# Order tables step by step, one pass for both contexts' tails, direct maxima in the last tile, expert biases on DVE: an eight-tile fp32r transformer block on one Trainium2 core

## What is computed

```python
# first block
nx = layer_norm(x)
evidence = softmax(nx @ Wq @ (ctx @ Wk).T / 16) @ (ctx @ Wv)
combined = concat(nx, evidence, cond)                  # 768 wide
probs = softmax(combined @ router_W + router_b)        # 3 experts
h = silu(combined @ e_w1[e] + e_b1[e])                 # 512 wide each
routed = sum_e probs[e] * (h @ e_w2[e] + e_b2[e])
g = sigmoid(silu(combined @ gate_w1 + gate_b1) @ gate_w2 + gate_b2)
x = x + g * (routed @ out_w + out_b)
# second block: 16 heads of width 16 over the 154 context tokens
q = ada_ln(x, cond) @ Wq + bq ;  k, v = split(ada_ln(ctx, cond) @ Wkv + bkv)
x = x + softmax(q @ k.T / 4) @ v @ Wp + bp
```

## Time and profile before

| quantity | value |
|---|---|
| runs, us | 566.02, 567.95, 571.80; median 567.95 |
| profiled execution | 570.17 us, of which the span from first to last instruction is 568.30 |
| busy in the span | PE 475.6, PEld 425.1, DVE 284.8, ACT 208.5, POOL 180.0 us |
| mean granted TensorE clock | 0.919 of full speed |
| mean of one instruction | tanh (L813) 598 ns, high half (L821) 620 ns, low half (L1303) 1298 ns, DVE product (L1161) 686 ns |
| one addition of 128x256 on POOL (L1353) | 0.72 us |

### The profile page before, as it was taken

One profiled execution on the slowest core, in us unless ns is written; L12 is line 12 of the kernel. 1 busy time (PEld: TensorE's weight loads), 2 busy tenths in 40 slices (PEclk: granted clock), 3 DMA queues, 4 the chain that ended last, 5 costly groups with the idle time before them and its releaser, 6 DMA issues.

```text
span 568.3 us, 9457 instructions
## 1 busy us (share of the span) xinstructions
PE 475.6 (84%) x3572; PEld 425.1 (75%) x3572; DVE 284.8 (50%) x717; ACT 208.5 (37%) x436; POOL 180.0 (32%) x167
## 2 busy tenths in 40 slices
PE   3998995959999978999889899979997999675563
PEld 2877895948988877878878787879787988652433
DVE  4536337673763574237733872494257426526212
ACT  1342331235346324532355227522741362142050
POOL 0653411063252434214522353424243122201111
PEclk9998997979999989999999999978996999768686
DMA  8376001320200112232001000200010001002000
GB/s 280 103 295 241 10 1 37 79 57 8 49 3 23 36 38 77 80 89 74 20 23 38 20 22 5 49 6 22 13 45 0 23 22 36 21 2 52 24 0 20
DMA packets 20608, 29.03 MB, mean 51 GB/s; under 512 B 4818, under 2 KB 17618, under 8 KB 20308
## 3 DMA queue, kind: packets, MB, share of 16 engines
q1 hardware_dynamic: 19264, 24.49, 14.1%
q0 software_dynamic: 1008, 3.67, 2.0%
q10 hardware_dynamic: 292, 0.28, 0.3%
HBM read 17.87 MB, written 2.10 MB: 35 GB/s over the span
## 4 chain that ended last, share of the span: by engine, by line
PE 51%; DVE 19%; issue 16%; ACT 6%; POOL 5%; DMA 2%; SPq 1%; POOLq 0%; ACTq 0%; DVEq 0%
PE hidden_banks L1368 4%; PE hidden_banks L1375 4%; PE hidden_banks L1370 4%; PE hidden_banks L1369 4%; PE score_banks L1677 3%; PE score_banks L1375 3%; DVE head_maxima L1221 3%; PE value_bank L1693 3%; PE token_bank L1368 3%; PE value_bank L1696 2%; PE token_bank L1369 2%; PE token_bank L1370 2%; PE score_banks L1654 2%; DVE router_logits L1147 2%; DVE hidden L1161 2%
## 5 line engine op out<-in xcount | busy, mean ns | idle before, releaser
L1303 POOL TENSOR_TENSOR hidden_low<-hidden,hidden_high 128x512 fp32r<-128x512 f32 x56 | 72.7, 1298 | 160.3 <-ACT hidden_high L821 160.2
L1221 DVE TENSOR_REDUCE head_maxima<-score_banks 128x2 f32<-128x308 f32 x128 | 55.1, 474 | 42.1 <-PE score_banks L1654 41.9
L1368 PE MATMUL hidden_banks<-normed_high,hidden_w_high 128*128 128x256 f32 x224 | 68.1, 304 | 3.3 <-DVE context_w_tail L922 2.7
L875 ACT ACTIVATE exp_ring<-score_banks 128x512 f32<-128x512 f32 x96 | 52.8, 601 | 38.5 <-PE score_banks L1677 38.2
L1368 PE MATMUL token_bank<-expert_out_high,hidden_high 128*128 128x256 f32 x192 | 58.7, 306 | 8.6 <-issue 7.2
L1369 PE MATMUL hidden_banks<-normed_high,hidden_w_low 128*128 128x256 f32 x224 | 64.3, 287 | 0.0
L1370 PE MATMUL hidden_banks<-normed_low,hidden_w_high 128*128 128x256 f32 x224 | 64.2, 287 | 0.0
L1161 DVE SCALAR_TENSOR_TENSOR hidden<-hidden,hidden_banks 128x512 f32<-128x512 f32 x56 | 38.4, 686 | 50.5 <-ACT hidden L813 49.6
L1654 PE MATMUL score_banks<-pair_keys,query_stack 96*128 96x308 f32 x128 | 39.8, 372 | 25.5 <-DVE head_maxima L1221 17.9
L1369 PE MATMUL token_bank<-expert_out_high,hidden_low 128*128 128x256 f32 x192 | 56.5, 294 | 0.0
L1370 PE MATMUL token_bank<-expert_out_low,hidden_high 128*128 128x256 f32 x192 | 56.4, 294 | 0.0
(11 more groups left out here) (209 smaller groups left out, 1146.7 us busy)
## 6 DMA issues: line engine op xcount, KB each, us to landing
unit_weights<-units SPq DMA_DIRECT2D x7, 768.0 KB, 5.1
query_stack<-queries_high SPq DMA_DIRECT2D x128, 32.0 KB, 1.9
w_slice<-units POOLq DMA_DIRECT2D x7, 512.0 KB, 3.9
tokens<-x SPq DMA_DIRECT2D x8, 256.0 KB, 7.1
query_stack<-queries_low SPq DMA_DIRECT2D x64, 32.0 KB, 1.9
out<-tokens SPq DMA_DIRECT2D x8, 256.0 KB, 2.2
w_T<-folds SPq DMA_DIRECT2D x1, 1536.0 KB, 8.5
pair_keys<-keys_high SPq DMA_DIRECT2D x32, 38.5 KB, 1.9
```

The costliest lines, as they stand in the source:

```text
L875: nc.scalar.activation(E[:, w % ERING, :], S[:, ring_of[key][0], :], ACT.Exp).then_inc(scalar_score, 1)
L1221: v.tensor_reduce(MX[:, s, :, c], S[:, ring_of[key][0], 0:2 * CTX].rearrange("p (j n) -> p j n", j=2), AX.X, ALU.max).then_inc(vector_most, 1)
L1303: nc.gpsimd.tensor_tensor(SL[:, ring(t, u), :], TB[:, ring(t, u), :], raw(SH[:, ring(t, u), :]), ALU.subtract).then_inc(gpsimd_h, 1)
L1368: mm(out_, lh, rh, start=start, stop=False, skip_group_check=skip)
```

## The change

- **Order tables.** `PLAN`, `PLAN_OF` (by tile) and `SETUP` give each step a slot of its own; `DELAY` has numbers of its own for the last tile. The first tile starts at slot 5 instead of 12.
- **Loads and start.** The first load holds context 0 and the value weights alone; four dummy matmuls (`warm`) stand before the first real one. Second weights come in six loads. The batch 1 slices are loaded by SP instead of POOL.
- **Context tails.** A new step `vt` computes, once per unit and for both batch entries, the tails with 32-column weights, and separately the condition's row; `context_w` keeps the first 128 tokens only. For batch entry 1 it uses the score banks' ring.
- **Keys.** The constant rows come by one DMA per batch entry; keys and queries are copied two pairs at a time (12 and 4 x 3 DMAs). Context x_hat moves from DVE to POOL.
- **Router.** ACT subtracts the maximum by its bias and makes the sum; the subtraction and the sum leave DVE.
- **Expert biases.** `bias2` makes each expert's bias once as a tile. From the third tile on `init` starts the sum of experts on DVE with bias x probability, and the bias matmuls are left out, except for the gate's.
- **Outputs.** A stream shuffle doubles the outputs (`dup`) so that high and low half share a tile of 128 rows; DVE makes the low half instead of POOL; `proj` has 2 matmuls a group and one bias matmul per half. Tile 6 and tile 7 use tiles and banks of their own.
- **Last tile.** `unstack` copies the keys back while its experts run; `most` multiplies the queries (high and low) by them with three 32-row matmuls, without the stack; the maxima go into the scores by a selection matrix (one matmul more per score) and not by DMA; rows, sums and outputs are made in two halves, tokens are stored in two parts. `fill` places 14 groups of four dummy matmuls.

```diff
-FIRST = 12
+FIRST = 5
+PLAN = {
+    "dup": (36.6, 40.5), "za": -0.51, "step": 1.99, "z": 0.3, "h": 1.5, "p": 3.33, "again": -9.3, "vw": -56.6,
+    "ln": -0.16, "norm": 1.7, "low": 11.8, "att": 7.8, "prob": 9.2, "route": 12.1, "logit": 15.01, "res": 17.8,
...
+    "most": (21.9, 22.1, 23.6, 25.2, 25.5, 26.9, 27.4, 28.1), "row": (29.46, 39.8), "stack": (13.9, 16.4, 17, 18.6),
...
+            def context_tail(key):
...
+                for k in range(KC):
+                    for b in range(BATCH):
+                        mm(tail_bank(u)[32 * b:32 * b + 32, 0:UCOLS], LT[b][:, k, :], U[:, u % URING, KC + k, :],
+                           start=(k == 0), stop=(k == KC - 1))
+                    for b in range(BATCH):
+                        last = mm(tail_bank(u)[64 + 32 * b:96 + 32 * b, 0:UCOLS], CO[:, k, b:b + 1].to_broadcast([P, 32]),
+                                  U[:, u % URING, 2 * KC + k, :], start=(k == 0), stop=(k == KC - 1))
...
             def logit(key):
-                nc.scalar.activation(PR[:, t % 2, :, :], LG[:, :, :], ACT.Exp).then_inc(scalar_logit, 1)
+                for s in range(NSUB):
+                    last = nc.scalar.activation(PR[:, t % 2, s, :], LG[:, s, :], ACT.Exp, bias=RT[:, 0, s:s + 1],
+                                                accum_out=RT[:, 1, s:s + 1])
...
+            def init(key):
...
+                for e in range(EXPERTS):
...
+                    for s in range(NSUB):
+                        p, bias = PR[:, t % 2, s, e:e + 1], BX[:, e, :] if e < 2 else BX3[:, :]
+                        if e == 0:
+                            last = v.tensor_scalar(ACC[:, s, :], bias, p, None, ALU.mult)
+                        else:
+                            last = v.scalar_tensor_tensor(out=ACC[:, s, :], in0=bias, scalar=p, in1=ACC[:, s, :],
+                                                          op0=ALU.mult, op1=ALU.add)
...
-                        if u % 2 == 0 and i == 1:
+                        if u % 2 == 0 and i == 1 and (t < PLAIN or u == 0):
                             last = mm(bank, BSEL[:, j:j + 1].to_broadcast([P, P]), CB[:, :], start=False, stop=True, skip_group_check=True)
...
             def most(key):
...
+                if t == LAST:
...
+                    exact(bank, (QH[rows, f, columns], QL[rows, f, columns]), (keys_high, keys_low), True, True).then_inc(tensor_most, 1)
+                else:
+                    mm(bank, QS[0:STACK, c, P * s:P * s + P],
+                       KS[b][0:STACK, c, :, :].rearrange("p j n -> p (j n)"), start=True, stop=True).then_inc(tensor_most, 1)
...
+            def proj_part(t, s, groups):
...
+                for g in groups:
+                    mm(proj_bank(t, s), both[:, g, c], WPh[:, g, :], start=(g == 0), stop=False)
+                    last = mm(proj_bank(t, s), both[:, g, c], WPl[:, g, :], start=False, stop=(g == GROUPS - 1))
```

More of the change, by code:

```diff
@@ L225 @@
+    "gpsimd": {
+        "h": 0.6, "ln": 0.8, "qn": -0.2, "low": 1, "keyn": 1.4, "split": 1.9,
+    },
+    "sync": {
+        "query": 10.5, "row": -4.5, "proj": -3.6, "last": 0.5, "key": -0.2, "place": 10.8, "query_last": 6.1,
+        "row_last": -1.7, "stack_last": -2.6,
+    },
 }
 LOOP = 2 * NU
-P_LAG = 3.3
 AGAIN = TPB - 1
-LN_AT, NORM_AT, LOW_AT, ATT_AT, PROB_AT, ROUTE_AT, LOGIT_AT = 0.5, 1.2, 3.2, 7.8, 9.3, 10.7, 12.4
-RES_AT, QN_AT, SHIFT_AT, XHAT_AT, QX_AT, QLOW_AT, QUERY_AT = 2.0, 2.1, 2.9, 3.0, 3.2, 5.2, 5.8
@@ new lines, in schedule @@
+    place(0, ("cv", 0), ("ck", 0), ("cv", 1))
+    for name in ("ln", "silu", "group", "gsplit", "setup2", "bias1", "cb", "bq"):
+        place(SETUP[name], (name, 0))
+    for u in range(NU):
+        place(SETUP["unit"][u], ("unit", u))
+        place(SETUP["vw"][u], ("vw", 0, u))
+        place(SETUP["vt"][u], ("vt", u))
+    for name in ("norm", "low", "att", "prob", "route", "logit"):
+        place(SETUP[name], (name, 0))
+    for u in range(1, NU):
+        place(SETUP["w2"][u - 1], ("w2", u))
@@ new lines, in schedule @@
+    place(SETUP["ck"], ("ck", 1))
+    for i in range(MODS):
+        place(SETUP["mod"][i], ("mod", i))
+    for i in range(2):
+        for name in ("late", "split", "keyn", "keyx", "key", "fold"):
+            place(SETUP[name][i], (name, i))
+    for name in ("sel", "unstack"):
+        place(SETUP[name], (name, 0))
+    for i in range(2):
+        place(SETUP["bias2"][i], ("bias2", i))
+    for i in range(FILLS):
+        place(SETUP["fill"][i], ("fill", i))
+    for t in range(NT):
+        at = FIRST + LOOP * t
@@ L295, in block1 @@
         for h in range(2):
-            place(at + RAW_AT[h], ("raw", t, h))
-            place(at + SUM_AT[h], ("sum", t, h))
-        place(at + SUMS_AT, ("sums", t))
-        place(at + OUT_AT, ("out", t))
-        place(at + OUTL_AT, ("outl", t))
-        place(at + PROJ_AT, ("proj", t))
-    place(0, ("setup", 0), ("load", 0), ("ctx", 0), ("fold", 0), ("ln", 0), ("silu", 0), ("group", 0))
-    place(1.5, ("bias1", 0), ("gsplit", 0))
-    for u in range(NU):
-        place(2 + u, ("unit", u), ("vw", 0, u))
@@ L336, in schedule @@
+        for h in range(parts_of(t)):
+            for name in ("row", "dup", "sums", "out", "outl"):
+                place(at + plan(t, name)[h], (name, t, h))
+        place(at + plan(t, "proj"), ("proj" if t < LAST else "lead", t))
+        if t == LAST:
+            for i in range(2):
+                place(at + plan(t, "last")[i], ("last", i))
+        elif t + SLOTS < NT:
+            place(at + plan(t, "reload"), ("reload", t))
     return table
 def order(engine):
-    placed = [(slot + DELAY[engine].get(key[0], 0.0), key) for slot, key in schedule()]
+    delays = DELAY[engine]
@@ L355, in ring_users @@
 def ring_users():
-    users = [key for key in order("tensor") if key[0] in ("most", "row", "score")]
+    users = [key for key in order("tensor") if key[0] in ("most", "row", "score") or key[0:2] == ("vw", 1)]
     return {key: (n % MRING, users[n - MRING] if n >= MRING else None) for n, key in enumerate(users)}
@@ L1231, in sums @@
[L1231 to L1242 removed]
+                t, h = key[1:]
```

1159 lines of the change are left out of this document (735 added, 424 removed).

## The result

The changed kernel takes 464.8 us (median of four runs, 463.8 to 467.3) where the kernel before takes 569.4 in the same comparison; the ratio is 0.817 (95% interval 0.812 to 0.823). The forecast was 465 us. The sum is right to the microsecond, and two of its four stages are wrong by 20 and 26 us, in opposite directions. So the total agrees by luck and proves nothing about the steps; the stages come first.

A forecast was written before the change was run, and what follows sets the result against it. Tiles 1 to 6 were bound by matmul count and short stops, the tail by a chain, the preparation by both. 101.1 + 279.2 + 40.4 + 44.6 = 465.3 us, plus 1.9 around it, 467.2; adjusted to the runs' median, 465; range 438 to 502.

The forecast's parts named there:

- A: Preparation and tile 0, up to tile 1's gate matmuls: 101.1 us instead of 127.4, bounds 88 to 114.
- (2): Preparation: dummy matmuls spare the first forty matmuls' slow start, -2.7 us; tail: tile 7's maxima take 8.7 us instead of 18.0.
- (4): Preparation: constant key rows become one DMA each, -8.7 us; tail: tile 7's scores and values take 10.5 us, before 10.2.
- B, the certain part: Tiles 1 to 6: fewer output-projection and expert-bias matmuls and no batch 1 context tails in tile 3, -19.7 us.
- B (5): Tiles 1 to 6: PE's stops at head maxima behind the stalled router subtraction shrink, idle 27.0 to 11 us, -16.
- The lock: Rival, chance 0.07: DVE's new two-input instructions hold POOL's hidden_low through the shared port pair, +15 us, 480.
- B (6): Tiles 1 to 6: less time at half clock once the stops are gone, -6 us (0 to -9).
- C: Tile 7's experts: 40.4 us instead of 46.5, bounds 37 to 45.
- D: Tail after tile 7's last expert matmul: 44.6 us instead of 73.5, bounds 39 to 56.
- The stops come back: Rival, chance 0.16: in tiles 1 to 6 head maxima wait behind other DVE steps, only 19.7 us go there, 487 us.
- Tight: Rival, chance 0.18: nearly no idle time left in tiles 1 to 6 (267 us), 438 us in all.
- Slower: Rival, chance 0.04: the relay between hidden and expert matmuls shows 2.0 us in each of 56 units, 577 us.

## Why the prediction was right in sum and wrong in its parts

- **A, 101.1 against 96.3.** First matmul forecast at 4.5, measured at 4.95 (at 4.30 without warming). The steps that fail are (2) and (6). The warming matmuls, -2.7 in the sum, are worth 0.3 us at most. The clock, -3 in the sum, went from 0.93 to 1.00: 7% of 127 us, up to 9 us. (4) and (5) hold together: apart from the start PE is idle 5.5 us, where the sum left 6.5.
- **B, the certain part.** 19.7 us of matmuls: their rows are gone; six bias matmuls, put back, cost 0.5 us a tile where I took 0.7.
- **B (5), the stops, -16.** Idle time fell from 27.0 to 1.4 us, -25.6, past my bound of -24. I had put the stops down to the stalled subtraction, "in every tile", and given the tables a small share. That is a misreading: the rows show one instruction in front of one wait, and of the 14.8 us of waits only 4.2 stood behind it. The lock is real and is worth 2% by itself, but nearly three quarters of the waits for the maxima outlive it. The places of the output chain and the maxima on DVE are what counted, and only the tables moved these.
- **B (6), the clock, -6.** 0.96 to 1.00 of 320.9 us is about 13. I had priced half clock and idle time as two terms with ranges of their own, though in this stage the half clock came and went with the stops. That is why B came out below my lower bound of 265: 320.9 - 19.7 - 25.6 - 13 gives 263, and 259.4 was measured; the last 3 us are not accounted for.
- **C, 40.4 against 36.1.** Below its bound of 37, and for the same reason: clock 1.00 and 1.25 us of idle time where I left 2.
- **D, 44.6 against 70.4, above its bound of 56 and by my own criterion a failed forecast.** (1) 15.6 instead of 13: the chain of before stays as it was. (2) From the first direct product, 407.35 us, to the last maximum, 420.36, are 13.0 instead of 8.7, at half clock from 410 on. (3) 2.0, as forecast. (4) 29.2 instead of 10.5: the error of the forecast. I put 24 selection matmuls at 0.118 us each, and 16 us as the bound, from rows in which all neighbours have the same shape. With 96 rows in both, the stage costs 11 us, which is the forecast within 1 us. (5) 10.5 against 10.4.
- **Rivals.** "The stops come back" is not what happened, but what the old slots would have done, and at three times its price of 22 us.
- **The lock.** hidden_low isn't held up, it takes 1299 ns on average in B and 1292 before. But DVE's new low part does hold POOL where they meet, in three tiles, from the timelines of the changed kernel:

```profile
216.87 1.27 DVE L1507 SCALAR_TENSOR_TENSOR outs_low<-outs_high,constants,outs_twice 128x1024 fp32r<-128x1024 f32 x1
217.04 1.67 POOL L1535 TENSOR_TENSOR rstd<-mean_var,minus_half 128x2 f32<-128x2 f32 x1
```

rstd takes 0.71 us in the other tiles. So the second half of the rule that the Trainium skill gives in "SBUF — State Buffer", section "SBUF: two separate sides", is seen in this trace too, 2.9 us of POOL's time in B; it cost PE nothing, because no matmul waited for it.
- **The other rivals.** "Tight", 438: B was tighter than this rival gave; D, 31 us above its 39, and A, 4 us above its 92, kept the time above it; with the shape mended the kernel takes 446.7. "Slower": no relay shows, PE's idle time in B is 1.4 us in all. "Doesn't do what it says" is true of the warming matmuls and of most fillers (those of the closing gain 1.0 us in the trace), and cost nothing.

The unsettled part is the clock between 407 and 423 us. In all six kernels looked at there it falls to half 3 to 8 us after tile 7's query matmuls, whether PE is idle there (the stack) or not (direct products), with and without fillers. What it falls on was not separated.

## What to carry to other kernels

Before a matmul of few rows is put between others of many, try it padded with zeros to their row count: 40 rows padded to 96 were worth 18 us here. In a kernel bound by PE a stop of PE can cost its length and nearly as much again by the clock (0.7 to 1.0 us per us in these four kernels). And when one stalled instruction stands in front of a wait, look at every wait of that kind and at what the in-order queue has in front of each, before the whole sum is booked to it: the timeline of the kernel before would have told, and undoing that one instruction did.

## What had not been expected of the hardware

- Matmuls of 96 and 40 rows in turn: 0.31 us from start to start at full clock and 0.51 at half, against 0.118 and 0.21 for equal rows and the same columns.
- The clock fell to half in the midst of back-to-back matmuls, all but two of 32 rows, 2.7 us after they began (407.35 to 410.0 us), with PE never idle.
- Dummy matmuls before the first load gained nothing: eight records take 3.6 us and end at 4.95 us, after the data has landed (4.30 us).
- POOL's rstd on two columns takes 1.67 us instead of 0.71 when it starts 0.17 us after DVE's outs_low.
